# The end of a graph network's last layer: GpSimd's share of the gated blend given to the projection, VectorE and ScalarE

## The reference, cut to what matters

```
h = relu(layernorm(x))
q, k, v = h @ Wq + bq, h @ Wk + bk, h @ Wv + bv
out = attention of q, k, v over the neighbours, 4 heads of 32, columns ordered (c, h)
x_r = h @ Ws + bs
beta = sigmoid(concat[out, x_r, out - x_r] @ Wb)          # Wb is 384 x 1
x = x + beta * x_r + (1 - beta) * out
```

## Time and profile before

| | us |
|---|---|
| median of three runs | 1574.15 |
| the three runs | 1573.74, 1581.84, 1574.15 |
| the profiled execution, its own time | 1577.51 |
| its span, first to last instruction | 1575.9 |
| GpSimd busy | 880.5 |
| VectorE busy | 945.1 |
| TensorE busy | 1022.1 |
| ScalarE busy | 675.9 |

### The profile page before, as it was taken

The page is one execution under the profiler, slowest core; times in us unless marked ns, Lnnn a source line. Parts: engine busy times, 40 slices in busy tenths (PEclk is TensorE's granted clock), DMA queues, the critical chain, the costliest instruction groups (busy, mean ns, idle before and its releaser), DMA issues.

```text
span 1575.9 us, 28816 instructions
## 1 busy us (share of the span) xinstructions
PE 1022.1 (65%) x6426; PEld 653.1 (41%) x6426; DVE 945.1 (60%) x2396; ACT 675.9 (43%) x2756; POOL 880.5 (56%) x1008
## 2 busy tenths in 40 slices
PE   0977987987883414556556469982747777777730
PEld 0534534543442304455445444441535455544520
DVE  3697797797786234555555660004446766777786
ACT  4994544554500302333333350001636666676650
POOL 3006677577787666666666506674045555555573
PEclk9998897897896556555655579995969999999985
DMA  8544665765512643455344876844333345333431
GB/s 289 235 162 154 211 209 155 209 217 164 206 57 63 156 94 92 104 107 108 103 105 109 90 263 244 308 151 38 109 100 104 96 95 106 92 103 98 96 42 53
DMA packets 97840, 216.43 MB, mean 137 GB/s; under 512 B 23222, under 2 KB 64058, under 8 KB 92154
## 3 DMA queue, kind: packets, MB, share of 16 engines
q1 hardware_dynamic: 66330, 126.87, 23.2%
q0 software_dynamic: 30304, 72.24, 23.2%
q10 hardware_dynamic: 1152, 16.78, 2.7%
HBM read 180.35 MB, written 32.13 MB: 135 GB/s over the span
## 4 chain that ended last, share of the span: by engine, by line
issue 29%; PE 26%; DVE 22%; POOL 7%; DMA 5%; DVEq 5%; ACT 3%; another core or an unknown queue 3%; SPq 1%; ACTq 0%; POOLq 0%
PE ps L1482 8%; POOL work L658 5%; DVE work L1180 3%; PE ps L1466 3%; DVE work L1311 3%; DMA work<-kv_table,stage 3%; PE ps L1623 2%; ACT unread L768 2%; PE ps L1632 2%; PE ps L1540 2%; PE ps L1442 1%; PE ps L1500 1%; DVEq L398 1%; DVE work L1176 1%
## 5 line engine op out<-in xcount | busy, mean ns | idle before, releaser
L658 POOL DMA_INDIRECT work<-h_table,stage x296 | 284.3, 960 | 190.1 <-issue 94.7
L658 POOL DMA_INDIRECT work<-kv_table,stage x204 | 194.5, 953 | 215.0 <-PE ps L1642 113.9
L768 ACT ACTIVATE unread<-work 128x128 bf16<-128x128 f32 x768 | 225.7, 296 | 145.4 <-DMA work<-in_adj_rows 140.0
L607 POOL DMA_INDIRECT work<-in_adj_rows,stage x192 | 246.2, 1282 | 73.2 <-issue 52.1
L1482 PE MATMUL ps<-work,h_sb 128*128 128x512 f32 x512 | 246.6, 638 | 36.8 <-ACT h_sb L722 36.8
L1311 DVE CUSTOM_DVE_ANT_0 work<-ps,work 128x512 f32<-128x512 f32 x200 | 140.8, 748 | 54.8 <-remote 19.8
L1482 PEld LDWEIGHTS ps<-work,h_sb 128*128 128x128 f32 x512 | 102.8, 206 | 166.1 <-issue 166.1
L768 ACT ACTIVATION_READ_ACCUMULATOR unread<-work 128x1 f32 x768 | 144.0, 187 | 0.0
L854 ACT ACTIVATE work<-work 128x512 f32<-128x512 f32 x197 | 139.8, 714 | 4.2 <-DVE work L1320 3.9
L1632 PE MATMUL ps<-ident,work 128*128 128x128 f32 x776 | 117.1, 288 | 31.0 <-DVE work L1327 22.9
L1540 PE MATMUL ps<-ident,work 128*128 128x128 f32 x196 | 51.3, 413 | 114.9 <-DVE work L1180 65.8
(11 more groups left out here) (213 smaller groups left out, 1979.9 us busy)
## 6 DMA issues: line engine op xcount, KB each, us to landing
work<-in_adj_rows SPq DMA_DIRECT2D x36, 2048.0 KB
work<-adj_table SPq DMA_DIRECT2D x74, 256.0 KB
work<-in_adj_rows ACTq DMA_DIRECT2D x8, 2048.0 KB
adj_table<-work POOLq DMA_DIRECT2D x102, 128.0 KB
mask_table<-work SPq DMA_DIRECT2D x51, 128.0 KB, 3.1
work<-mask_table SPq DMA_DIRECT2D x51, 128.0 KB
work<-h_table,stage POOLq DMA_INDIRECT x296
kv_table<-work SPq DMA_DIRECT2D x32, 128.0 KB
```

What stands on the lines that cost most here:

```text
L607: nc.gpsimd.indirect_dma_start(out=ag[:, h, c, :], out_offset=None, in_=adj_rows, in_offset=bass.IndirectOffsetOnAxis(ap=stage[:, h // 2, ...
L658: nc.gpsimd.indirect_dma_start(out=rows[:, b, c, :], out_offset=None, in_=table, in_offset=bass.IndirectOffsetOnAxis(ap=stage[:, b, c:c + ...
L768: ins = nc.scalar.activation(unread[:, m % (MQ // 2) * TB + t, :], ring[:, q, m, t * P:(t + 1) * P], ACT.Abs, accum_out=seen[:, b, t, q * ...
```

## The change

The third weight matrix and its bias get one column more: W_s (w2 - w3) and b_s (w2 - w3). The projection then gives x_r·(w2 - w3) as column 129 of x_r, so `h_sb` becomes the first 128 columns of a wider tensor `h_wide` with rows of 129. The weight rows and the column are made by VectorE ahead of layer 2's list loop, and TensorE waits for them (`wb_ready`) before each product of the projection of layer 3. VectorE adds x_r to x for all four groups at the start of layer 3, ahead of the list loop. In the end part VectorE also makes out - x_r, ScalarE multiplies it by 1/(1 + exp(z)) with eight scaled copies for a group (`scale`), and VectorE adds x + x_r (`blend`); the last group is multiplied and added by VectorE itself, tile by tile (`blend_tiles`). GpSimd has nothing left to do behind its last gather. `work` shrinks from 31240 to 30592 columns, and the tile `ag` in it moves down.

```
-FIN_LINKS = 1 + 7 * GROUPS
+FIN_LINKS = 1 + 4 * GROUPS
...
-        h_sb = sb("h_sb", [P, T, P])
+        h_wide = sb("h_wide", [P, T, P + 1])
+        h_sb = h_wide[:, :, 0:P]
...
-        zed3, xz = (work[:, 29956 + T * n:29956 + T * (n + 1)] for n in range(2))
+        zed3 = work[:, 29956:29956 + T]
+        xz = h_wide[:, :, P:P + 1]
...
-            pool.wait_ge(wb_ready, 1)
-            pool.wait_ge(post_done[3], T)
-            for i in range(GROUPS):
-                rows = xr[:, FT * i:FT * i + FT, :]
-                wait(pool, xz_ready, i - 1)
-                nc.gpsimd.tensor_tensor(xw[:, i % 2, :, :], rows, wide_row(wb_bc[:, P:2 * P]), ALU.mult).then_inc(xw_ready, 1)
-            for i in range(GROUPS):
-                rows = slice(FT * i, FT * i + FT)
-                nc.gpsimd.tensor_tensor(x_sb[:, rows, :], x_sb[:, rows, :], xr[:, rows, :], ALU.add).then_inc(xs_ready, 1)
-            pool.wait_ge(xs_ready, GROUPS)
-            for i in range(GROUPS):
-                rows = slice(FT * i, FT * i + FT)
-                pool.wait_ge(link_e[3], turned_out(i))
-                nc.gpsimd.tensor_tensor(xr[:, rows, :], fin[:, i, :, :], xr[:, rows, :], ALU.subtract).then_inc(dif_ready, 1)
...  ScalarE
-            def row_sums(i):
-                ...
+            def scale(i):
+                act.wait_ge(gate_ready, i + 1)
+                for j in range(FT):
+                    ins = nc.scalar.activation(fin[:, i, j, :], fin[:, i, j, :], ACT.Copy,
+                                               scale=zed3[:, FT * i + j:FT * i + j + 1])
+                ins.then_inc(scaled, 1)
...
+            for i in range(GROUPS):
+                exps_of(i)
+                if i < GROUPS - 1:
+                    scale(i)
...  VectorE, projection
-                        ins = nc.vector.tensor_tensor(xr[:, t, :], ps[:, bank, 2 * P:3 * P], bkvs_bc[:, 2 * P:3 * P], ALU.add)
+                        ins = nc.vector.tensor_tensor(h_wide[:, t, :], ps[:, bank, 2 * P:3 * P + 1],
+                                                      bkvs_bc[:, 2 * P:3 * P + 1], ALU.add)
...  VectorE, ahead of layer 2's list loop
+            nc.vector.tensor_tensor(wb_bc[:, 0:P], wb_bc[:, 0:P], wb_bc[:, 2 * P:3 * P], ALU.add)
+            link(nc.vector.tensor_tensor(wb_bc[:, P:2 * P], wb_bc[:, P:2 * P], wb_bc[:, 2 * P:3 * P], ALU.subtract))
+            for n, rows in enumerate((wkvs_sb, bkvs_bc)):
+                ins = nc.vector.tensor_tensor_reduce(out=junks[:, n, :], in0=rows[:, 2 * P:3 * P], in1=wb_bc[:, P:2 * P], scale=1.0,
+                                                     scalar=0.0, op0=ALU.mult, op1=ALU.add,
+                                                     accum_out=rows[:, 3 * P:3 * P + 1])
...  VectorE, outputs(i)
                     link(nc.vector.tensor_tensor(prodw, out_of(i), wide_row(wb_bc[:, 0:P]), ALU.mult))
+                    if i:
+                        gate_of(i - 1)
                     link(nc.vector.tensor_reduce(zeds(i), prodw, AX.X, ALU.add))
-                    dve.wait_ge(xz_ready, i + 1)
-                    nc.vector.tensor_tensor(zeds(i), zeds(i), xz[:, FT * i:FT * i + FT], ALU.add).then_inc(z_ready, 1)
+                    nc.vector.tensor_tensor(sums, sums, xz[:, tiles, :], ALU.add).then_inc(z_ready, 1)
+                    nc.vector.tensor_tensor(out_of(i), out_of(i), xr[:, tiles, :], ALU.subtract)
+
+                def gate_of(i):
+                    dve.wait_ge(ez_ready, i + 1)
+                    link(nc.vector.tensor_scalar(zeds(i), zeds(i), 1.0, None, ALU.add))
+                    nc.vector.reciprocal(zeds(i), zeds(i)).then_inc(gate_ready, 1)
 
                 def blend(i):
-                    ...
+                    dve.wait_ge(scaled, i + 1)
+                    nc.vector.tensor_tensor(x_sb[:, tiles, :], out_of(i), x_sb[:, tiles, :], ALU.add).then_inc(fin_ready, 1)
+
+                def blend_tiles(i):
+                    dve.wait_ge(gate_ready, i + 1)
+                    for j in range(FT):
+                        t = FT * i + j
+                        ins = nc.vector.scalar_tensor_tensor(x_sb[:, t, :], fin[:, i, j, :], zed3[:, t:t + 1], x_sb[:, t, :],
+                                                             ALU.mult, ALU.add)
+                    ins.then_inc(fin_ready, 1)
...
-                blend(GROUPS - 1)
+                gate_of(GROUPS - 1)
+                blend_tiles(GROUPS - 1)
...  VectorE, start of layer 3 (lines 1395 and 1396 go)
+            dve.wait_ge(post_done[3], T)
+            for i in range(GROUPS):
+                tiles = slice(FT * i, FT * i + FT)
+                nc.vector.tensor_tensor(x_sb[:, tiles, :], x_sb[:, tiles, :], xr[:, tiles, :], ALU.add).then_inc(xs_ready, 1)
...  TensorE, multiply
-                        mm(ps[:, bank, 0:3 * P], rows, wkvs_sb[:, :], start=True, stop=True)
+                        pe.wait_ge(wb_ready, 1)
+                        mm(ps[:, bank, 0:3 * P + 1], rows, wkvs_sb[:, :], start=True, stop=True)
```

More of the change, by code:

```diff
@@ L93, in build @@
         bq_sb = sb("bq_sb", [P, 1])
-        wkvs_sb = sb("wkvs_sb", [P, 3 * P])
-        bkvs_bc = sb("bkvs_bc", [P, 3 * P])
+        wkvs_sb = sb("wkvs_sb", [P, 3 * P + 1])
+        bkvs_bc = sb("bkvs_bc", [P, 3 * P + 1])
         wb_bc = sb("wb_bc", [P, 3 * P])
@@ L106, in build @@
         half_neg = sb("half_neg", [P, 1])
-        work = sb("work", [P, 31240])
+        work = sb("work", [P, 30592])
         tri = sb("tri", [P, P], BF16)
@@ L161, in build @@
         inv = work[:, 23040:23044]
-        ag = work[:, 30216:31240].rearrange("p (h c n) -> p h c n", h=4, c=HALF)
+        ag = work[:, 29568:30592].rearrange("p (h c n) -> p h c n", h=4, c=HALF)
         onehot = work[:, 23048:27144].bitcast(F16).rearrange("p (b s m) -> p b s m", b=2, s=P)
@@ L183, in build @@
         mk = work[:, 16896:17920].bitcast(BF16).rearrange("p (b n) -> p b n", b=NBUF)
-        junk = work[:, 24704:24832]
+        junks = work[:, 24704:24960].rearrange("p (n f) -> p n f", n=2)
+        junk = junks[:, 0, :]
         kvrow = work[:, 6656:7680].rearrange("p (b f) -> p b f", b=TB)
@@ L255, in build @@
         wb_ready = sem("wb_ready")
[L256 to L259, removed]
+        gate_ready = sem("gate_ready")
+        scaled = sem("scaled")
+        fin_ready = sem("fin_ready")
         z_ready = sem("z_ready")
@@ L300, in build @@
         link_u = sem("link_u")
+        link_w = sem("link_w")
+        xs_ready = sem("xs_ready")
         NLD = 15
@@ L343, in wide_row @@
             return v.rearrange("p (a f) -> p a f", a=1).to_broadcast([P, FT, P])
[L345 to L351, removed]
         class Quad:
@@ L547, in _ @@
             for i in range(GROUPS):
-                sp.wait_ge(link_e[3], blended(i))
+                sp.wait_ge(fin_ready, i + 1)
                 sp.dma_start(out[FT * P * i:FT * P * (i + 1), :].rearrange("(t p) f -> p t f", p=P),
@@ L1263, in step2 @@
                 settle(dve)
+            link = Link(dve, link_w, 1)
+            nc.vector.tensor_tensor(wb_bc[:, 0:P], wb_bc[:, 0:P], wb_bc[:, 2 * P:3 * P], ALU.add)
+            link(nc.vector.tensor_tensor(wb_bc[:, P:2 * P], wb_bc[:, P:2 * P], wb_bc[:, 2 * P:3 * P], ALU.subtract))
+            link.end()
+            for n, rows in enumerate((wkvs_sb, bkvs_bc)):
+                ins = nc.vector.tensor_tensor_reduce(out=junks[:, n, :], in0=rows[:, 2 * P:3 * P], in1=wb_bc[:, P:2 * P], scale=1.0,
+                                                     scalar=0.0, op0=ALU.mult, op1=ALU.add,
+                                                     accum_out=rows[:, 3 * P:3 * P + 1])
+            ins.then_inc(wb_ready, 1)
             nc.vector.memset(acc[:, T:T + 1, :], 0.0).then_inc(state_reset[2], 1)
@@ L1360, in outputs @@
                     tiles = slice(FT * i, FT * i + FT)
+                    sums = zeds(i).rearrange("p (t a) -> p t a", a=1)
                     link(nc.vector.tensor_tensor(out_of(i).rearrange("p t (c h) -> p t h c", h=H),
@@ L1365, in outputs @@
                     link(nc.vector.tensor_tensor(prodw, out_of(i), wide_row(wb_bc[:, 0:P]), ALU.mult))
+                    if i:
+                        gate_of(i - 1)
                     link(nc.vector.tensor_reduce(zeds(i), prodw, AX.X, ALU.add))
-                    dve.wait_ge(xz_ready, i + 1)
-                    nc.vector.tensor_tensor(zeds(i), zeds(i), xz[:, FT * i:FT * i + FT], ALU.add).then_inc(z_ready, 1)
+                    nc.vector.tensor_tensor(sums, sums, xz[:, tiles, :], ALU.add).then_inc(z_ready, 1)
[4 more added lines that the diff above has]
+                    nc.vector.reciprocal(zeds(i), zeds(i)).then_inc(gate_ready, 1)
                 def blend(i):
                     tiles = slice(FT * i, FT * i + FT)
[L1372 to L1378, removed]
+                    dve.wait_ge(scaled, i + 1)
[7 more added lines that the diff above has]
+                    ins.then_inc(fin_ready, 1)
```

(4 more changed lines are left out.)

1 line of the change is left out of this document (removed).

## The result

| | before | changed |
|---|---|---|
| median of nine runs each | 1578.85 us | 1560.24 us |
| the runs, lowest to highest | 1569.34 to 1585.19 | 1548.86 to 1566.79 |
| the profiled execution: own time, span | 1577.51, 1575.9 | 1558.83, 1556.5 |

The ratio is 0.9882 with a 95% interval of 0.9855 to 0.991. On the median of before that is 18.6 us less, where 18.6 was forecast.

A forecast was written before the change was run, and what follows sets the result against it. It took the end part's chain over VectorE and GpSimd as the bound, with VectorE also held while GpSimd runs. Net 20.1 - 1.1 - 0.4 = 18.6 us, so 1574.15 - 18.6 = 1555.6 us, range 1550 to 1566.

The forecast's parts named there:

- VectorE is held by GpSimd's reads: End part: two-input VectorE instructions in SBUF stand still while GpSimd runs, 3.34 us in place of 1.23 for an addition.
- slow by itself: Rival: product 1365 is slow from its broadcast row, not the lock; 7.3 us lost, 1562.9 us, chance 0.05.
- The end part: From the reciprocal's start to VectorE's last end: 32.53 us, with VectorE ending at 1552.2 in place of 1572.3.
- The groups: End part, groups 1 to 3: 7.49 us each plus 0.1 of waiting for ScalarE's copies, in place of 10.2.
- The updates by tile: Last group of the end part: eight VectorE tile updates, 2.17 us.
- ScalarE as the bound: Rival: the end part's scaled copies do not overlap, waiting 2.1 us in place of 0.3; 1557.4 us, chance 0.08.
- The start of the end part: First reciprocal, ahead of group 0: follows ScalarE's last exponential, starting at 1519.67 in place of 1520.74, 1.07 us won.
- The gathers: Start of layer 3: moved additions delay the first gathers by 1.1 us (bounds 0 and 1.6), taken in full.
- The projection's column: Layer 3's projection: one column more in 64 matmuls costs 0.1 us; with the waits 0.4 together.
- the waits: Layer 3's projection: a long-met wait before each of 32 products, taken as 0.3 us, at most 1.0 in all.
- the wider rows: Dense layers: weight loads at steps of 129 elements stay hidden, cost nothing; rival of slower loads 1605 us, chance 0.03.
- layer 2's start: Ahead of layer 2's lists: about 1.3 us of added VectorE work hidden in 15.02 us of idling, costing nothing.

The follow-up runs named there:

- e5: Changed kernel plus twelve GpSimd products of 128 x 1024 that nobody waits for, issued behind the last gather; end part 42.30 us.
- e6: Changed kernel plus twelve GpSimd memsets of 128 x 2048, which write and read nothing, behind the last gather; end part 33.57 us.
- e8: Changed kernel with the last group also scaled by ScalarE's eight copies and added by one VectorE instruction; end part 33.79 us.
- e7: Changed kernel with the gate product of groups 0 to 2 on VectorE in place of ScalarE's scaled copies; end part 35.96 us.
- e11: Changed kernel with feature sums of groups 0 to 2 moved from VectorE to ScalarE; end part 28.05 us, ratio to before 0.9884.
- e3: Changed kernel without the four additions of x_r to x (output lacks that share); first gather 0.98 us, end part 32.28 us.
- e9: Changed kernel unaltered, compared with the kernel before a second time; ratio 0.9919 (0.9888 to 0.995), end part 32.29 us.
- e10: Changed kernel with x_r added to x tile by tile inside layer 3's projection, timed; ratio to before 0.9899 (0.987 to 0.9929).
- e12: Changed kernel with feature sums on ScalarE and x_r added tile by tile in the projection; ratio to before 0.9855, median 1554.02 us.
- e1: Kernel before with only h_sb's rows widened to 129 elements (ag moved down to make room); ratio to before 0.9993 (0.9955 to 1.003).

## Why the prediction was right

Step by step, as it stood on record:

- *VectorE is held by GpSimd's reads.* Shown by e5 (10.0 us beside 23.6 us of GpSimd work that nobody needs) and narrowed by e6 (writes alone do not hold the two-input instructions). The product that had never been seen alone takes 1.23 us, so the rival "slow by itself" falls.
- *The end part.* The sum was 32.53 us for a measured 32.28. The groups were 7.49 plus 0.1 of waiting for a measured 7.53; the waiting was 0.09. The updates by tile took 2.19 for 2.17, and e8 puts the other way at 1.5 us more.
- *ScalarE as the bound.* Falls: e7 pays 3.7 us without it, and e11 gives it as much work again at no wait.
- *The start of the end part.* Here a term was mis-sized. The prediction let the reciprocal start 0.13 us behind ScalarE's last exponential and won 1.07 us. It started 0.89 us behind it (1519.71 to 1520.60), where it had been 1.20: 0.3 us won. The row names VectorE's own last instruction of the list as what came last, 0.54 us before the reciprocal; in this execution its rescaling stood at 1519.17, behind a copy of its own. In eleven of the fourteen traces the reciprocal stands 0.41 to 0.55 us behind that instruction's end, a distance that the prediction did not count. When the list happens to be early, as in e3, the reciprocal follows the exponential's end at 1439.04 by 0.10 us. The step looked at one neighbour and not at VectorE's own queue.
- *The gathers.* The hold was sized at 1.1 and measured at 2.01 - 0.98 = 1.03, but the sum was right and its parts were not: 0.2 was taken for the first gather and 1.0 for the second, and the first was held for 1.03 and the second not at all. The hold was taken to go through to the end. Whether it does can't be told. From the first gather to the reciprocal are 379.1 us before and 378.8 after. In the later sets on the same chip as e9 they are 375.8 (e9), 377.4 (e11), 383.4 (e7) and 385.1 (e8) with the gather held, and 375.5 (e10) and 378.8 (e12) with it free. Anything below several us is lost in that scatter. What might absorb it was not tested; right behind it stands the stall of ScalarE that the earlier trace rows shows at 1162.39, and in the changed trace ScalarE's second copy of keys comes at 1155.58, with stalls of 3.46 us (VectorE, until 1164.70) and 5.51 us (ScalarE, until 1165.51) behind it.
- *The projection's column, the waits, the wider rows, layer 2's start.* The projection takes 38.4 us before and 38.5 after (0.4 was charged, and it varies by 1 us anyway). e1 shows the weight loads unchanged by the wider rows and no cost in the total. VectorE still idles 13.96 us ahead of layer 2's first list (15.02 before), so the work there is hidden.

So the mechanism was right, and that the total was hit to a tenth of a us was luck. In the profiled pair, whose own times are 18.7 us apart, the end part won 0.25 us more than forecast, the start of the end part 0.9 less (0.14 in place of 1.07), the 1.5 charged for gathers and projection do not show, and the time outside the span grew by 0.7 (1.6 to 2.3); the four cancel. The second comparison (e9) gave 10 to 13 us. The runs do not tell 18.6 from several us less.

The page "SBUF — State Buffer" of the Trainium skill (section "Who interferes with whom") says that a VectorE instruction with two inputs in SBUF contends with a GpSimd instruction that reads SBUF and not with one that only writes, and that tensor_scalar can enter a mode in which it contends with GpSimd. The traces agree: 2.88 us for the product beside e5's products and 1.23 beside e6's memsets, and 1.37 for a tensor_scalar beside a memset (e6). The page's inference that tensor_tensor leaves descriptor generation alone does not help with an indirect DMA: 2.01 us beside the additions, 0.98 without them (e3). That instruction also reads its index column (`stage`) from SBUF, and which part of it is held, no run shows.

## What to carry to other kernels

Where VectorE's instruction is much longer beside a busy GpSimd than its like elsewhere (here 2.88 to 3.40 us for 1.23), count the difference as GpSimd's cost even if nobody waits for its result; giving the work to ScalarE, to a spare column of a matmul or to an idle stretch removes both. Size a serial end part from start-to-start distances of rows with the same shape, which here gave 32.5 for 32.3 us. When a wait goes, check the waiting engine's own last instructions too before crediting it. Compare the total in a second set of runs before trusting a close hit: the end part repeated to 0.01 us, the gain in the total did not repeat to 5. Once the end part is one engine's busy time, each instruction moved off it counts in full (e7, e11), as long as the order gives the other engine a group's time to answer.

## What was not expected of the hardware

A tensor_scalar of 8 columns, next to nothing by itself (0.17 us), took 1.37 us beside GpSimd's memsets (e6) and 1.95 beside its products (e5), while the reciprocal of the same eight columns took 0.20 in both. GpSimd's two-input instructions on 128 x 1024 took 2.34 us with rows of 128 elements and 2.17 with rows of 129 (e1, e5). And a GpSimd indirect DMA waits out the one VectorE addition that is running and is then served, although four stand back to back: it was held for 1.03 us and not for the 2.3 us that the additions still ran. In e8 it began a little later in its addition and was held for less, 0.87 us, and in both traces it ended 0.84 to 0.86 us behind that addition's end. In e8:

```profile
1145.89 1.22 DVE L1406 TENSOR_TENSOR x_sb<-x_sb,h_wide 128x1024 f32<-128x1024 f32 x1
1146.10 1.85 POOL L653 DMA_INDIRECT work<-kv_table,stage  x1 [47.63 <-DMA kv_table<-work]
```
